# Storing the layer 1 rows of a block in one transfer of 8 KB per row, in place of four of 2 KB

## The reference, cut to what matters

```python
h = relu(layernorm(x))
feat_all = einsum('ni,rhid->rnhd', h, conv_weights)        # layer 0: a row per node and type
alpha = softmax over the edges of a target of leaky_relu(el + er)
x = x + segment_sum(alpha * feat_all[type, src], dst) + h_bias
h = relu(layernorm(x))
h_all = einsum('ni,rio->nro', h, einsum('rb,bio->rio', comp, basis))   # layer 1: a row per node and type
agg = segment_sum(h_all[src, type], dst)
x = x + layernorm(gelu(agg + h @ loop_w + h_bias + h)) * gamma + beta
```

## Time and profile before

| what | value |
|---|---|
| median of three runs | 2796.43 us (2791.49 to 2800.01) |
| span of the profiled execution | 3432.1 us, 26416 instructions |
| own time of the profiled execution beside its span | none is given: the span, from the first to the last instruction, is all there is |
| mean granted clock of TensorE in it | 0.735 |
| busy in the span: PE, PEld, DVE, ACT, POOL | 57%, 41%, 45%, 19%, 59% |
| DMA | 403.12 MB in 168505 packets, 117 GB/s on average |

### The profile page before, as it was taken

One profiled execution on the slowest core, in us unless ns is written; L12 is line 12 of the kernel. 1 busy time (PEld: TensorE's weight loads), 2 busy tenths in 40 slices (PEclk: granted clock), 3 DMA queues, 4 the chain that ended last, 5 costly groups with the idle time before them and its releaser, 6 DMA issues.

```text
span 3432.1 us, 26416 instructions
## 1 busy us (share of the span) xinstructions
PE 1960.6 (57%) x8092; PEld 1402.3 (41%) x8092; DVE 1538.5 (45%) x3220; ACT 667.0 (19%) x1202; POOL 2024.5 (59%) x2138
## 2 busy tenths in 40 slices
PE   7873536666665666566575772544544434554445
PEld 6772324444443444344453441333333322333334
DVE  6763546555655555455565540222332322323324
ACT  4423122333332323233323120000000000000001
POOL 6736555655555555555655527666666666666663
PEclk9985667788787878787787895666666766666667
DMA  8455334444443444444443333233333333333332
GB/s 229 158 189 174 103 98 119 128 132 130 131 136 111 138 122 128 120 129 120 135 133 112 97 129 104 84 93 93 98 98 92 97 92 100 96 95 98 97 92 70
DMA packets 168505, 403.12 MB, mean 117 GB/s; under 512 B 49741, under 2 KB 75820, under 8 KB 160682
## 3 DMA queue, kind: packets, MB, share of 16 engines
q0 software_dynamic: 95312, 261.58, 28.1%
q1 hardware_dynamic: 73050, 139.85, 11.8%
HBM read 325.41 MB, written 75.86 MB: 117 GB/s over the span
## 4 chain that ended last, share of the span: by engine, by line
PE 36%; another core or an unknown queue 28%; DVE 19%; issue 13%; ACT 1%; DVEq 1%; POOL 1%; DMA 0%; ACTq 0%; POOLq 0%
PE PB L1844 20%; PE PB L1955 6%; DVE ACC L1328 5%; DVE Z L1356 5%; PE PB L1796 4%; PE PB L1919 3%; DVE OHZ L1538 2%; DVE ERM L1337 1%; DVE OHZ L1346 1%; PE PB L1960 1%; POOL Z L841 1%; PE PB L1903 1%; DVEq L1315 0%; PE PB L1958 0%
## 5 line engine op out<-in xcount | busy, mean ns | idle before, releaser
L841 POOL DMA_INDIRECT Z<-tab,KI x1963 | 1868.2, 952 | 1260.0 <-issue 560.2
L1844 PE MATMUL PB<-Z,OHZ 128*128 128x260 f32 (+1 forms) x3926 | 1190.0, 459 | 808.0 <-issue 522.9
L1844 PEld LDWEIGHTS PB<-Z,OHZ 128*128 128x128 f32 x3926 | 861.5, 229 | 1085.3 <-issue 668.6
L1328 DVE TENSOR_TENSOR ACC<-ACC,PB 128x260 f32 (+1 forms) x997 | 421.4, 423 | 1493.4 <-remote 1031.1
L1919 PE MATMUL PB<-pick,ERM 128*128 128x16 f32 (+1 forms) x504 | 113.3, 375 | 476.2 <-DVE ERM L1337 440.4
L1919 PEld LDWEIGHTS PB<-pick,ERM 128*128 128x128 f32 (+1 forms) x504 | 109.9, 330 | 489.9 <-DVE ERM L1337 452.8
L1356 DVE TENSOR_TENSOR Z<-Z,PB 128x2048 f32<-128x2048 f32 (+1 forms) x125 | 283.9, 2271 | 0.0
L1955 PE MATMUL PB<-w,ht 128*128 128x512 f32 x480 | 271.5, 729 | 1.8 <-ACT ht L1714 1.8
L1776 ACT ACTIVATE ACC<-ACC 128x256 f32<-128x256 f32 x30 | 10.4, 406 | 857.2 <-DVE ACC L1328 857.2
L1955 PEld LDWEIGHTS PB<-w,ht 128*128 128x128 f32 x480 | 112.2, 241 | 139.0 <-issue 136.4
L1796 PE MATMUL PB<-wh,hx 128*128 128x424 f32 (+1 forms) x500 | 152.2, 375 | 20.7 <-DVE hx L933 15.7
(11 more groups left out here) (333 smaller groups left out, 1498.4 us busy)
## 6 DMA issues: line engine op xcount, KB each, us to landing
OHZ<-dlt SPq DMA_DIRECT2D x31, 1024.0 KB
Z<-tab,KI POOLq DMA_INDIRECT x1963
tab<-st SPq DMA_DIRECT2D x120, 256.0 KB
tab<-Z SPq DMA_DIRECT2D x24, 1040.0 KB, 4.3
TD<-typ SPq DMA_DIRECT2D x31, 256.0 KB
tab<-Z SPq DMA_DIRECT2D x5, 1024.0 KB, 8.1
xn<-xb SPq DMA_DIRECT2D x30, 128.0 KB
X<-xn SPq DMA_DIRECT2D x6, 640.0 KB
```

What stands on the lines that cost most here:

```text
L841: pool.indirect_dma_start(to, None, tab, at).then_inc(d_fe[g % 2][part(g, k) * layer], 16)
L1328: dv.tensor_tensor(a, a, bank(done + i)[:, 0:width], ALU.add).wait_op(*previous, "sem-ge").then_inc(*o.of(s_add))
L1844: last = pe.matmul(p, OH[:, slot, k + i, :], rows_, start=(i == 0), stop=(i == n - 1))
```

## The change

For blocks 0 to 24 (r < WHOLE = 25) SP waits for the last quarter and stores all four quarters with one transfer of 128 rows x 8 KB on the semaphore `d_st[0]`. Blocks 25 to 29 are stored in four quarters as before. `stored(r, j)` gives the semaphore and the count that say that quarter j of block r - 1 has landed; ACT, POOL and SP wait by it. The whole `ST1` of a partition is 8 KB in one piece, and so is a node's row of `tab1`. Nothing is added or removed on the other engines.

```diff
+        WHOLE = NG - 7
...
+        def stored(r, j):
+
+            if r <= WHOLE or j == 0:
+                return d_st[0], 16 * r
+            return d_st[j], 16 * (r - WHOLE)
...
             def store_table(r):
 
                 t = block_rows(sp, SYE, r, tab1p)
+                if r < WHOLE:
+                    sp.wait_ge(s_ev, moved(r, 3))
+                    sp.dma_start(t, ST1[:, :, :].rearrange("p j n -> p (j n)")).then_inc(d_st[0], 16)
+                    return
                 for j in range(4):
                     sp.wait_ge(s_ev, moved(r, j))
                     sp.dma_start(t[:, 512 * j:512 * j + 512], ST1[:, j, :]).then_inc(d_st[j], 16)
...
-                sp.wait_ge(d_st[j], 16 * NB)
+                sp.wait_ge(*stored(NB, j))
...
-                pool.wait_ge(d_st[j], 16 * NB)
+                pool.wait_ge(*stored(NB, j))
...
                 if r:
-                    ac.wait_ge(d_st[j], 16 * r)
+                    ac.wait_ge(*stored(r, j))
                 ac.activation(ST1[:, j, :], quarter_bank(j)[:, :], ACT.Copy).then_inc(*o.of(s_ev))
```

## The result

The changed kernel takes 2801.82 us in the median of 13 runs (2798.33 to 2806.89), the kernel before 2796.43 us (2791.16 to 2800.28, 13 runs). The ratio is 1.0019, with a 95% interval of 1.0011 to 1.0026: some 5 us slower. The time lies in the forecast's range and within the 0.3% called "same", but the interval leaves 1 out. So there is a small loss to explain, where the prediction had none.

The account below looks back on a forecast made before the run. The prediction took a chain over several engines to bound the kernel. Its terms (issues, transfer size, later start, what lies behind the store) were each 0, leaving the median at 2796 us, range 2777 to 2815 us (forecast's own 2788 to 2805).

Parts of the forecast that it names:

- The issues, 75 fewer: SP's store issues, three fewer per block for 25 blocks: 25.8 us of SP time, none on a path, gain 0.
- The transfer's size: One 1 MB store per block instead of four quarters: 4.3 us from issue to landing, no engine waits, cost 0.
- rival 4: The 8 KB rows are cut into 2 KB pieces again: forecast time, packets would not fall; chance 0.03 within no change.
- What lies behind the store, `xb`, masks and targets: Loads queued behind the larger store: `xb` up to 2.3 us later, targets issued after the store is over; cost 0.
- Rival 2: The large store delays targets or early gathers: at most 75 us slower (2871 us), at a quarter 19 us; chance 0.09.
- The gathers: POOL's gathers share DMA engines with the store; those meeting it are read some 50 us later, so cost 0.
- rival 1: Quarter stores leaving the tail of a group's gathers let them land sooner: up to 38 us faster (2759 us); chance 0.11.
- The span is 635.7 us longer than the median: Profile span of 3432.1 us against the median: slack shown in the profile may be smaller in a run.
- no engine is busy for more than 59%: Whole span of the profile: the time is made by a chain over several engines and not by one.

Follow-up runs that it names:

- e18_null: The kernel before, unchanged, timed against itself and profiled on an occasion when it takes some 2796 us: 2798.5 us, ratio 1.0000.
- padded set: Four kernels with an extra POOL fill after each layer 0 gather, each group's first gather waiting for DVE's previous read; only stores of blocks 0 to 24 differ: 3396.31 to 3455.46 us.
- e15: Kernel before with POOL padded in layer 0, whole stores of blocks 0 to 24 issued right with the group's last gather: 3455.46 us, +59.2 us against e14.
- e14: Kernel before with POOL padded in layer 0, stores in four quarters at their usual place; reference of the padded set: 3396.31 us, ratio 1.2147.
- e17: Kernel before with POOL padded in layer 0, whole stores of blocks 0 to 24 held until DVE has read the group: 3397.55 us, +1.2 us against e14.
- e16: Kernel before with POOL padded in layer 0, four quarter stores issued in a row from the last gather on: 3425.53 us, +29.2 us against e14.
- e19_after_read: The changed kernel with each whole store held until DVE has read the group's gathered rows: 2800.52 us, ratio 1.0010 to the kernel before.
- e11: The kernel before with less PE work, one of three score pieces and the first of two sum chunks: 3433.81 us, beside 3484.94 for the kernel before.

## Why the prediction was wrong, point by point

**The issues, 75 fewer: cost 0. Right.** SP still waits for DVE before the masks, 9.3 us per group (287.2 us over 31 waits, in the changed kernel's layer 0) against 8.9 in e18_null (277.1 over 31). The 4.3 us of the prediction are of the long pace.

**The transfer's size: 0 by itself, 4.3 us to landing. Right in its size.** It is 4.8 us on the page, where 4.3 was taken. The 20 quarters that are left take 2.0 us in the median, all 120 of e18_null 3.0 us. The queue has 10800 packets fewer; I had 9600. The rows make up 25 x (512 - 128) = 9600, and the other 1200 are packets of 4 bytes (5573 in e18_null, 4373 after), 16 for each of the 75 transfers fewer. So rival 4 is out. The queue's share is 14.6% of 2802.7 us against 14.3% of 2794.9, so the larger rows save no engine time: 409 against 400 us. The megabytes move at one rate, as said. That it is no gain was right.

**What lies behind the store, `xb`, masks and targets: 0. Right.** ACT's wait for the targets over layer 0 is 216.2 us (32 times) after and 216.1 us in e18_null. Rival 2 in the form in which it was priced, by late targets, is refuted.

**The gathers: "DVE first reads the group at 1234.75, 18.7 us later. In all 32 groups DVE never waits there ... Cost 0." This is the step that failed.** At the pace of the runs the read is 2.8 us after the last gather's issue (up to 4.3 in the kernel before), and DVE waits there for the gather in 31 of 32 groups. The prediction had considered it: rival 1 reckoned with a slack that shrinks to 4.5 us and 2.5 us after the landing. It looked only at the first quarters that leave the tail, a gain, and not at the one large store that then falls into the tail of the same group. (The second of the two times that it gives for those stores, 1.8 us before the read, is 1.65 by the issue; nothing hangs on it.) Rival 2 had the large store delay gathers, but "early gathers", which are read 50 us later. The true loss combines the two: rival 2's mechanism at rival 1's place. The read is 2.2 us late in the padded set and 2.5 to 3.0 us here, and where every block meets and nothing hides it, 25 meetings cost 59 us. Here it came to 5.7 us, as the store lies in the half microsecond or so behind the last gather in four groups only, and as 1.2 us of each delay is slack. That the time stayed within the stated range is therefore luck of these distances, and not the cover that the prediction gave as its reason.

That the meetings are rare and regular is in the trace too. A meeting sets the next store back against the gathers, to 3.4 us after the last one in group 9. Then it moves forward again, over 3.2, 2.0, 1.5 and 1.9 us, and in group 14, at 0.6 us, it meets. The next six groups do the same. With the quarters the moves of ACT are spread over the tail: in e18_null a quarter lies near it in most groups, DVE reads 2.8 to 4.3 us after the last gather, and POOL has not waited beyond its issue gap. In groups 6 to 30 its reads are together 14.4 us later than 2.8 us each, more than the 10.9 us of the changed kernel, and cost nothing: many small delays stay below the slack, four large ones do not.

As to the mechanism, rival 2's picture holds in the packets, with one thing to add: the piece behind which the gather stands is not a row but a whole transfer's share of a DMA engine. The 128 rows of a store over 16 engines are eight each; at 0.31 us per row of 8 KB that is 2.5 us, and at 0.085 us per row of 2 KB 0.7 us for a quarter. In e15 the gather's first packet is 2.2 us late, and so is the read. Where the store goes out 0.4 to 0.6 us behind the gather the two are mixed: in group 14 of the changed kernel (0.57 us) the gather's packets start from 2.65 us on, most of them among those of the store, and the last ends at 5.3 us. Why they mix there is open. Long rows and large transfers were never set apart here, as no run stores 1 MB in short rows by one issue.

The Trainium skill (DMA: Bandwidth & Descriptors, Queues, rings and completion order) says that a DMA engine goes round its queues a whole packet at a time, and counts 9 to 17 descriptors as typical for one, so its packet is more than one packet record of the profile. The trace of e15 agrees: between the first and the last of the store's 128 rows no packet of the gather starts, in any of the 25 groups. The same section says that the write to the semaphore lands only after all earlier writes of that engine, of other queues too. That is not needed for the size of the delay: the gather's own last packet ends 2.1 us later (4.50 against 2.44), and the read is 2.2 us later.

**"The span is 635.7 us longer than the median", so that distances in it are stretched.** This is the root of the failed step. The excess was not the profiler's but the long pace, at which the kernel took 3432 to 3497 us on four occasions. With "no engine is busy for more than 59%", the prediction took the time for a chain over several engines. At the pace of the runs POOL is the bound, at 1.25 us per gather. The sign of it was in the rows: 0.95 us and 0.30 us to the next gather, 1963 times by the page, are 2454 us of the median's 2796. That sum would have shown POOL as the bound, and with it the last gather as the place to look at.

**The passage between the layers: not foreseen, and open.** 3.2 to 3.6 us of what the two kernels with whole stores lose in their profiles lies there, and the clock's rows show how. That whole stores cause the falls is not shown. In the padded set, too, the number of falls differs from kernel to kernel, and not with the whole stores: in e14 and e17 the clock stays up through the rest of the passage once it has risen (81.1 us both), in e15 it falls once (82.3 us) and in e16 twice (85.3 us). What brings them stays open, and each kernel has one profile here. The residual ratio of e19_after_read, 1.0010, is 2.8 us, about as large as its 3.2 us. It fits, and no more is claimed.

No version beat the kernel before. At the short pace e19_after_read comes nearest, and its interval begins just above 1.

## What to carry to other kernels

Before distances in a profile are used, set its span against the runs, and count the busiest queue by its own pace: so many gathers by start-to-start time. Where that nearly gives the median, this engine is the bound, and its last transfer of a group is the one that must not be late. Making a store larger is harmless only away from that transfer: look for the moment at which the merged store goes out. Here it did harm when it was issued 0.07 to 0.57 us behind a gather that somebody waited for, and none from 1.3 us on. If it falls there, let it wait until that gather is read.

## What the runs showed of the hardware that was not expected

The same program runs at two paces. In two sets the kernel before took 2796 to 2797 us, as in the runs of the result, and in four 3432 to 3497 us, with little spread within an occasion (3411.7 to 3446.97 in 29 runs). It is not the chip: one chip gave 3431.78 on one occasion and 2795.82 on another. In the traces of the long pace DVE stands some 10 to 15 us per group before it adds PE's sums ("remote", 263 to 347 us in 580 to 1950 us), and with a third of the scores and half of the sums left, e11 still ran at 3433.81. What holds the work then stays open.

A gather of 0.13 MB that is issued just before a store of 1 MB moves nothing until the last of the store's 128 packets has started: its own first packet starts at 3.8 us or later in place of 1.64 us, 25 times out of 25 in e15.

The granted clock fell to 1.2 GHz for 3.4 us, twice, in two of three kernels whose PE did the same work in the same order. Ahead of both falls PE had been busy for 1.4 of 4 us in the changed kernel, and for 1.4 and 1.8 us in e19_after_read; in e18_null, without a fall, for 1.7 and 1.9.
